# Node products of a four-layer graph network with several rows to one product

## The reference

```python
# layer two (attention): agg3 = mean * aw[0] + max * aw[1] + sum * aw[2]
ef = edge_label @ trans_weight                 # 8 labels to 64
att = sigmoid(leaky(x[row] * x[col] @ attention_weight) + leaky(ef @ edge_attention_weight))
out, opinion = agg3(x[col] * att, row), agg3(ef * att, row)
inn, inn_opinion = agg3(x[row] * att, col), agg3(ef * att, col)
cat = concatenate((out, opinion, inn, inn_opinion), axis=1)
y2 = cat @ weight + bias
...
# layer three (graph convolutions with self loops, norm = dinv[row] * ew * dinv[col])
x2 = relu(segment_sum(norm * (x @ w1)[row], col) + b1)      # 64 to 16
x3 = relu(segment_sum(norm * (x2 @ w2)[row], col) + b2)     # 16 to 32
x4 = relu(segment_sum(norm * (x3 @ w3)[row], col) + b3)     # 32 to 64
y3 = concatenate([x, x4], axis=1) @ lw + lb
```

## Time and profile before

| | |
|---|---|
| median of 3 runs | 15446.13 us (15444.47 to 15448.31) |
| the profiled execution's own time | 15444.99 us |
| its span, first to last instruction | 15443.3 us |
| mean granted TensorE clock | 0.689 |
| busy: POOL, DVE, PE | 70%, 59%, 47% of the span |
| products A, B, E, from the first transpose to the last result | 76.7, 34.6, 35.5 us |

### The profile page before, as it was taken

The page is one execution under the profiler, slowest core; times in us unless marked ns, Lnnn a source line. Parts: engine busy times, 40 slices in busy tenths (PEclk is TensorE's granted clock), DMA queues, the critical chain, the costliest instruction groups (busy, mean ns, idle before and its releaser), DMA issues. The chain is left out here.

```text
span 15443.3 us, 186434 instructions
## 1 busy us (share of the span) xinstructions
PE 7260.8 (47%) x53190; PEld 4887.6 (32%) x53190; DVE 9169.8 (59%) x21286; ACT 2508.3 (16%) x6533; POOL 10805.1 (70%) x10524
## 2 busy tenths in 40 slices
PE   3333333333320010001001355886787999699997
PEld 2222222222210000000000113786786555444443
DVE  5555554444444444444444796665665777587776
ACT  2222212222210000000000232111111111122222
POOL 6777777777767777777777301677777777588886
PEclk6555555555555555555555565998998999699998
DMA  2222223333323333333333574121211222122222
GB/s 81 70 71 72 71 64 95 103 103 101 103 83 94 94 99 94 93 99 94 93 97 96 202 272 149 39 44 37 43 43 36 48 49 50 26 72 72 71 73 60
DMA packets 631953, 1295.15 MB, mean 84 GB/s; under 512 B 219505, under 2 KB 366134, under 8 KB 606402
## 3 DMA queue, kind: packets, MB, share of 16 engines
q1 hardware_dynamic: 279776, 776.44, 14.4%
q0 software_dynamic: 337792, 456.35, 13.8%
q10 hardware_dynamic: 14337, 61.82, 1.1%
HBM read 623.75 MB, written 671.67 MB: 84 GB/s over the span
## 5 line engine op out<-in xcount | busy, mean ns | idle before, releaser
L521 POOL DMA_INDIRECT rows<-spline_table,index x3136 | 3181.4, 1014 | 1097.5 <-issue 973.9
L880 POOL DMA_INDIRECT rows<-gcn_table,index x2548 | 2515.9, 987 | 1008.1 <-issue 720.5
L920 PE MATMUL p_slots<-part,one_lo 128*128 128x208 bf16 (+1 forms) x25872 | 2973.8, 278 | 449.5 <-DVE one_lo L938 449.4
L920 PEld LDWEIGHTS p_slots<-part,one_lo 128*128 128x128 bf16 x25872 | 2372.6, 98 | 1050.2 <-DVE one_lo L938 492.9
L1116 POOL DMA_INDIRECT sent<-a_msg,a_place x1568 | 1625.9, 1037 | 478.0 <-issue 477.7
L1108 POOL DMA_INDIRECT a_rows<-att_table,a_index x1568 | 1486.2, 948 | 484.7 <-issue 477.2
L1170 PE MATMUL a_p_score<-tw_att,a_label 128*128 128x16 f32 x196 | 59.0, 381 | 3632.0 <-DMA a_label_row<-in_label_rows 3632.0
L1484 POOL DMA_INDIRECT e_rows<-soft_table,e_index x1176 | 1468.8, 1249 | 375.4 <-issue 328.8
L1526 PE MATMUL e_p_slots<-soft_part,e_one_lo 128*128 128x455 bf16 x8232 | 1644.7, 362 | 0.0
L1204 DVE TENSOR_TENSOR a_product<-a_rows,a_xdst 128x1024 f32<-128x1024 f32 x98 | 120.1, 1226 | 2067.2 <-DMA a_rows<-att_table,a_index 2067.2
L680 DVE TENSOR_TENSOR msg<-rows,weight 128x1024 f32<-128x1024 f32 x196 | 241.2, 1230 | 1814.2 <-DMA rows<-spline_table,index 1814.2
(11 more groups left out here) (430 smaller groups left out, 14929.7 us busy)
## 6 DMA issues: line engine op xcount, KB each, us to landing
running_dst<-a_run SPq DMA_DIRECT2D x98, 1600.0 KB
running_src<-s_run SPq DMA_DIRECT2D x98, 1600.0 KB
running<-e_run_rows SPq DMA_DIRECT2D x98, 656.0 KB
s_rows<-sent ACTq DMA_DIRECT2D x98, 584.0 KB, 7.0
keys<-key_rows SPq DMA_DIRECT2D x200, 256.0 KB, 3.3
running<-run SPq DMA_DIRECT2D x98, 520.0 KB
rows<-spline_table,index POOLq DMA_INDIRECT x3136
running<-run SPq DMA_DIRECT2D x98, 512.0 KB
```

The source lines that it names most:

```text
L521: pool.indirect_dma_start(out=rows[h][:, k, :], out_offset=None, in_=table, in_offset=offsets(index[h][:, k:k + 1])).then_inc(gathered[h], 16)
L880: pool.indirect_dma_start(out=rows[h][:, K + k, :], out_offset=None, in_=table, in_offset=offsets(index[h][:, k:k + 1])).then_inc(gathered ...
L920: ins = nc.tensor.matmul(to, one_lo[h][:, q, e:e + P], flat(part[:, q, :, :]), start=q == 0 and part_no == 0, stop=q == CLASSES - 1 and pa ...
```

## The change

`dense` gets a list `pack`, how many node rows of an input go to one product. For a pack of s it transposes s rows together (s times the width as columns) and multiplies with a weight tile that holds the weights s times on the block diagonal, so that one product gives s rows of the result side by side. Where seven isn't a multiple of s, the last block overlaps the one before it. A takes its label input seven rows at once (16 x 7 = 112 rows, 448 columns) and then adds the seven products of the other input, B and E take two rows (four blocks), C seven (one block, 112 rows, 224 columns), D four (two blocks, 256 columns). For this, 15 weight tiles' parts are loaded in place of 4, four tiles are cleared at the start, and the label weights are made on 112 rows and masked. `comb_lab` is no tile of its own any more but columns 184 to 199 of `agg_dst`, and `class_keys` uses columns 128 to 159 of each row of `agg_dst` as scratch.

```diff
-def dense(nc, sig, xs, weights, out, width, store=None, bias=None, block=None, scope=None, prepare=None, ready=0):
+def dense(nc, sig, xs, weights, out, width, store=None, bias=None, block=None, scope=None, prepare=None, ready=0, pack=None):
...
-        k_dims = [w.shape[0] for w in weights]
+        pack = pack or [1] * K
+        k_dims = [w.shape[0] // s for w, s in zip(weights, pack)]
+        starts = [[min(o, G - s) for o in range(0, G, s)] for s in pack]
...
-        xt = [sb(f"xt{k}_", [d, G, P]) for k, d in enumerate(k_dims)]
+        xt = [sb(f"xt{k}_", [s * d, len(o), P]) for k, (d, s, o) in enumerate(zip(k_dims, pack, starts))]
...
-                    ins = nc.vector.tensor_copy(flat(xt[k][b][:]), flat(tp[k][0:k_dims[k], 0:G, :]))
+                    ins = nc.vector.tensor_copy(flat(xt[k][b][:]), flat(tp[k][0:pack[k] * k_dims[k], 0:len(starts[k]), :]))
...
-                    for g in range(G):
-                        ins = nc.tensor.transpose(tp[k][0:k_dims[k], g, :], xin[k][b][:, g, :], sig["ident"][:])
+                    for m, o in enumerate(starts[k]):
+                        ins = nc.tensor.transpose(tp[k][0:pack[k] * k_dims[k], m, :], flat(xin[k][b][:, o:o + pack[k], :]), sig["ident"][:])
...
-                for g in range(G):
-                    for k in range(K):
-                        ins = nc.tensor.matmul(acc[b % ACCS][:, g, 0:width], xt[k][b][:, g, :], weights[k], start=(k == 0), stop=(k == K - 1))
+                to = acc[b % ACCS]
+                if K == 2 and pack[1] == G:
+
+                    nc.tensor.matmul(to[:, 0:G, 0:width], xt[1][b][:, 0, :], weights[1], start=True, stop=False)
+                    for g in range(G):
+                        ins = nc.tensor.matmul(to[:, g, 0:width], xt[0][b][:, g, :], weights[0], start=False, stop=g + 1 == G)
+                else:
+                    for m, o in enumerate(starts[0]):
+                        for k in range(K):
+                            ins = nc.tensor.matmul(to[:, o:o + pack[k], 0:width], xt[k][b][:, m, :], weights[k], start=(k == 0), stop=(k == K - 1))
...
-        w_ef, w_lab, twt = sb("w_ef", [C, 2, C]), sb("w_lab", [2 * LABELS, C]), sb("twt", [C, 3 * LABELS])
+        w_ef, w_lab, twt = sb("w_ef", [C, 2, C]), sb("w_lab", [GROUP_SLOTS * 2 * LABELS, GROUP_SLOTS, C]), sb("twt", [C, 3 * LABELS])
...
-        w1, w2, w3 = sb("gw1s", [C, 16]), sb("gw2s", [16, 32]), sb("gw3s", [32, C])
...
-        lws = [sb(f"lws{k}", [C, C]) for k in range(2)]
+        lws = [sb("lws0", [C, C])]
...
+        w1_two, w2_all, w3_four, lws1_two = sb("w1_two", [2 * C, 2, 16]), sb("w2_all", [GROUP_SLOTS * 16, GROUP_SLOTS, 32]), sb("w3_four", [P, 4, C]), sb("lws1_two", [2 * C, 2, C])
...
-            (w1[:], gw1), (w2[:], gw2), (w3[:], gw3), (gb[0][:], gb1.broadcast_to([P, 16])), (gb[1][:], gb2.broadcast_to([P, 32])),
-            (gb[2][:], gb3.broadcast_to([P, C])), (lws[0][:], lw[0:C, :]), (lws[1][:], lw[C:2 * C, :]), (lbs[:], lb.broadcast_to([P, C])),
+            *((w1_two[k * C:(k + 1) * C, k, :], gw1) for k in range(2)), *((w2_all[k * 16:(k + 1) * 16, k, :], gw2) for k in range(GROUP_SLOTS)),
+            *((w3_four[k * 32:(k + 1) * 32, k, :], gw3) for k in range(4)), (gb[0][:], gb1.broadcast_to([P, 16])), (gb[1][:], gb2.broadcast_to([P, 32])),
+            (gb[2][:], gb3.broadcast_to([P, C])), (lws[0][:], lw[0:C, :]), *((lws1_two[k * C:(k + 1) * C, k, :], lw[C:2 * C, :]) for k in range(2)), (lbs[:], lb.broadcast_to([P, C])),
...
-                    step(V.memset(w_labels[:], 0.0))
+                    for t in (w_labels, w1_two, w2_all, w3_four, lws1_two):
+                        step(V.memset(t[:], 0.0))
...
+                label_sides = [sb(f"label_side{k}", [C, GROUP_SLOTS, 2 * LABELS], F32, rows) for k in range(2)]
+                w_lab_at = sb("w_lab_at", [GROUP_SLOTS * 2 * LABELS, GROUP_SLOTS], F32, rows)
...
-                    TABLE, SHIFTED, DEGREES, MASKED = dve_s.base + 4, dve_s.base + 6, dve_s.base + 9, dve_s.base + 11
+                    LABEL_ROWS = GROUP_SLOTS * 2 * LABELS
+                    TABLE, SHIFTED, DEGREES, MASKED = dve_s.base + 4, dve_s.base + 6, dve_s.base + 9, dve_s.base + 14
...
-                        nc.tensor.matmul(ps[0:2 * LABELS, C:2 * C], twt[:, 0:2 * LABELS], w_ef[:, 0, :], start=True, stop=False)
-                        nc.tensor.matmul(ps[0:2 * LABELS, C:2 * C], twt[:, LABELS:3 * LABELS], w_ef[:, 1, :], start=False, stop=True).then_inc(pe_s.sem, 1)
+                        nc.tensor.matmul(ps[0:LABEL_ROWS, C:2 * C], flat(label_sides[0][:]), w_ef[:, 0, :], start=True, stop=False)
+                        nc.tensor.matmul(ps[0:LABEL_ROWS, C:2 * C], flat(label_sides[1][:]), w_ef[:, 1, :], start=False, stop=True).then_inc(pe_s.sem, 1)
...
+                        for k in range(2):
+                            step(V.tensor_copy(label_sides[k][:], repeat(twt[:, k * LABELS:(k + 2) * LABELS], GROUP_SLOTS)))
+                        step(V.tensor_reduce(w_lab_at[:], sig["ident"][0:LABEL_ROWS, 0:LABEL_ROWS].rearrange("p (k l) -> p k l", l=2 * LABELS), AX.X, ALU.add))
...
-                        step(V.tensor_copy(w_lab[:], ps[0:2 * LABELS, C:2 * C]))
+                        step(V.tensor_tensor(w_lab[:], repeat(ps[0:LABEL_ROWS, C:2 * C], GROUP_SLOTS), spread(w_lab_at[:], C), ALU.mult))
...
-            comb_dst, comb_lab = sb("comb_dst", [P, J, 2 * C], F32, tmp), sb("comb_lab", [P, J, 2 * LABELS], F32, tmp)
+            comb_dst = sb("comb_dst", [P, J, 2 * C], F32, tmp)
+
+            comb_lab = agg_dst[:, :, RUN - 2 * LABELS:RUN]
...
-                    in_class = flat(agg_dst[:])[:, 0:T]
-                    step(V.tensor_copy(src_key[:, 0:T], src_lo[:, 0:T]))
+                    def by_row(t):
+                        return t[:, 0:T].rearrange("p (j c) -> p j c", j=J)
+
+                    in_class, key, low, high = agg_dst[:, :, 2 * C:2 * C + T // J], by_row(src_key), by_row(src_lo), by_row(src_hi)
+                    step(V.tensor_copy(key, low))
...
-                        step(V.tensor_scalar(in_class, src_hi[:, 0:T], q * CLASS - 0.5, None, ALU.is_gt))
-                        step(V.scalar_tensor_tensor(src_key[:, 0:T], in_class, float(P * q), src_key[:, 0:T], ALU.mult, ALU.add))
-                        step(V.scalar_tensor_tensor(src_hi[:, 0:T], in_class, -float(CLASS * q), src_hi[:, 0:T], ALU.mult, ALU.add))
+                        step(V.tensor_scalar(in_class, high, q * CLASS - 0.5, None, ALU.is_gt))
+                        step(V.scalar_tensor_tensor(key, in_class, float(P * q), key, ALU.mult, ALU.add))
+                        step(V.scalar_tensor_tensor(high, in_class, -float(CLASS * q), high, ALU.mult, ALU.add))
...
-            dense(nc, sig, [comb_src, comb_lab], [w_src[:], w_lab[:]], y, C, bias=y)
+            dense(nc, sig, [comb_src, comb_lab], [w_src[:], flat(w_lab[:])], y, C, bias=y, pack=(1, GROUP_SLOTS))
...
-                dense(nc, sig, [agg[2]], [w3[:]], x4, C, bias=gb[2][:], block=block, scope=scope, prepare=own_part)
-
-            dense(nc, sig, [xs], [w1[:]], x2, 16)
+                dense(nc, sig, [agg[2]], [flat(w3_four[:])], x4, C, pack=(4,), bias=gb[2][:], block=block, scope=scope, prepare=own_part)
+
+            dense(nc, sig, [xs], [flat(w1_two[:])], x2, 16, pack=(2,))
...
-            convolve(1, second_table, lambda block, scope, own_part: dense(nc, sig, [agg[1]], [w2[:]], x3, 32, bias=gb[1][:], block=block, scope=scope, prepare=own_part))
+            convolve(1, second_table, lambda block, scope, own_part: dense(nc, sig, [agg[1]], [flat(w2_all[:])], x3, 32, pack=(GROUP_SLOTS,), bias=gb[1][:], block=block, scope=scope, prepare=own_part))
...
-            dense(nc, sig, [x4], [lws[1][:]], y, C, bias=y)
+            dense(nc, sig, [x4], [flat(lws1_two[:])], y, C, bias=y, pack=(2,))
```

## The result

| | before | after |
|---|---|---|
| median of the runs, us | 15447.22 (15444.47 to 15449.35, 4 runs) | 15351.72 (15347.81 to 15354.81, 4 runs) |
| profiled execution, us (its span) | 15444.99 (15443.3) | 15350.33 (15348.6) |

The ratio of the runs is 0.9938, with a 95% interval of 0.9921 to 0.9955: the changed kernel is faster by 95.5 us. The five products gave more than was forecast, and some 9 us of it did not reach the end.

What follows compares the result with a forecast made beforehand. TensorE was taken to bound A, B and E, the chain after the last gather C and D. Savings of 31.1 + 15.6 + 5.2 + 12.4 + 16.1 = 80.4 us gave 15366 us, range 15340 to 15397.

Steps and rivals of the forecast that it cites:

- A: Attention layer's sources product, w_src with w_lab; forecast to take 45.5 us, 31.1 saved.
- B: Product w1 at the graph layer's entry; forecast 15.6 us saved.
- E: Product lws[1] at the graph layer's end; forecast 16.1 us saved, or 15.4 if its 128-column records cost more.
- C: Product w2 beside the fetch, counted only after the last gather; forecast 5.2 us saved.
- D: Product w3 beside the fetch, counted only after the last gather; forecast 12.4 us saved.
- D's step that the gather takes the bound over: In the w3 product, the last gather, not TensorE, becomes late, so 12.4 us of 16 are saved.
- The price of a record at 0.50: TensorE's fp32 records at the low clock: 0.208 us up to 128 columns, 0.76 for 448, 0.43 for 256, 0.38 for 224.
- 22 x 0.208 + 2 x 0.76 = 6.10 us: Time per group in A after the change: 8 transposes, 14 w_src records and 2 wide label records.
- the clock rises: Rival: TensorE's clock goes up; A would lose 19 us more, B and E 8 each, giving 15331; 7%.
- three other rivals: Chain in series, 31 us lost, 9%; packed records priced as full, 81 us, 3%; long passes' gathers retimed, 15482 us, 3%.
- the chain in series: Rival: each multiply waits for its copy; B and E periods near 4, A 7.5, 31 us lost, 15397; 9%.
- What was costed at nothing: Slower class-key comparisons (2.4 us), eleven weight loads, four memsets, extra VectorE steps; all taken as hidden beside other work.

Runs made afterwards that it cites:

- b_wide: Changed kernel with B reading each weight column four times (128 columns a record, not 32); slower chip, 19019.44 us, ratio 0.9913; B 14.5 us.
- a_by_rows: Changed kernel with A as before the change, labels multiplied row by row; slower chip, 19048.22 us, ratio 0.9913; A 75.1 us.
- a_narrow_label: Changed kernel with A's labels still turned once for seven rows but multiplied row by row, 14 records of 64 columns; A 39.5 us.
- e_narrow: Changed kernel with E computing only 16 of 64 result columns, 32 columns a record instead of 128; E 18.9 us instead of 14.9.
- keys_flat: Changed kernel with the class keys' steps over flat tiles as before, comparison output contiguous; 15323.99 us against 15324.5.
- after_again: Changed kernel once more, unaltered, beside runs of the kernel before on one chip; 15324.5 us, ratio 0.9934.
- a_no_label: Changed kernel without A's two wide label-product records, labels still copied and transposed; A 24.5 us.
- more_packed: Changed kernel with the first layer's two w0 products on two rows at once and B reading weights four times; 15299.35 us, ratio 0.9919.

## Why the prediction came out as it did

- **What bounds the stages: right.** In A, B and E the engine without rest is TensorE before and after, C and D end by the chain behind the last gather. D's step that the gather takes the bound over shows in VectorE's 4.34 us of waiting; without that step 16 would have been forecast where 12.6 came.
- **The price of a record at 0.50: right.** A's group was put at 6.10 us and took 6.11 where the clock was still low (b_wide), B's at 2.50 and took 2.46; 224 and 256 columns were priced well enough for C to end 5.9 us after the last gather's issue (6.3) and D 8.9 (9). B, C and D missed by at most 0.5 us each. The wide pair of w_lab starts at 9571.99 and the next product at 9573.48: 0.75 us a record, where 0.76 had been taken. The 0.37 us for 448 columns, estimated from the formula for the low clock in the Trainium skill ("TensorE: Matmul & The Clock Gate", Back-to-back issue gap), is half of that for an fp32 record here.
- **A: the mis-sized term, by its clock.** 31.1 was forecast and 49.5 came. The step that failed is "22 x 0.208 + 2 x 0.76 = 6.10 us" for every group. It holds only at 0.50. In the profile the first period is 9575.13 - 9570.26 = 4.87 us, the clock rising in it, and the others 3.15: 1.2 and five times 3.0 us less, and 2 us less in the last multiply, make the 18. The prediction had seen records at both paces in the old A, and gave a rise throughout 7%. It did not foresee that the new A would hold the high clock where the old one kept falling back, which a_by_rows and a_narrow_label show.
- **E: the same, smaller.** 16.1 forecast, 20.6 measured, the period 1.5 us from the third group on. B was taken as evidence for E. It was none: B stays low with 32 columns a record and rises with 128, E rises with 128 and stays low with 32 (b_wide, e_narrow). The Trainium skill's "TensorE: Matmul & The Clock Gate", Part 1, says that a busy TensorE gets the full clock. E's two forms do not bear that out as the profile counts busy: in the first 7 us from the first transpose they are equally busy, 6.13 us with 128 columns and 6.12 with 32 (changed kernel, e_narrow), and only the first rose.
- **The rival *the clock rises* happened in half**: in A and E, not in B. Its conditions were tested against B alone. The three other rivals did not happen: the periods are TensorE's own sum, packed records of 128 columns cost 0.24 us, the long gathers' mean is 1014 ns before and after. The price given to the chain in series, 31 us, does not follow from its own periods: 12 of B and E at 1.5 us more and six of A at 1.4 make 26.
- **What was costed at nothing: right.** Comparisons take 1.79 us (1.8); the keys are sent at 9544.60, the last gather is at 9547.95: the cover of 7 us shrank to 3.4 and still covers. The 3 us either way on POOL came out as 1.3 us gained (keys_flat). The added weight loads end near 4420 instead of 4414, still ahead of the store at 4446.89, and the first cast of the opening starts at 10.14 instead of 10.05.
- **The sum against the whole.** 104.1 us in the stages, 94.7 in the span, 80.4 forecast. That a clock rising in part stays inside the range was reasoned. That the number came within 14 us was in part luck: the stages gave 23.7 us more than forecast, and the passes nobody edited took 9.4 longer. On the chip of after_again the medians differ by 101.8 us, 21 more than forecast. Most of those 9.4 lie in the softmax pass, which differs by more than that between two profiles of the changed kernel; the second pair, on one chip, leaves 2.6 us. That any of it belongs to the change was not shown.
- **Open.** What makes the clock rise in A's first multiply in one execution and in the second in another (27.15 and 29.6 us), and why the old A swings, was not settled. Nor was what decides for a rise in general: columns decided in B and E, but w_dst and a_no_label's A, so alike, went different ways.

## What to carry to other kernels

Price a product in the fp32 records that it issues: here, at the low clock, one of 32 or 64 columns cost 0.21 to 0.22 us and one of 128 only 0.24, so stacking small node rows into one tall operand with block-diagonal weights saves turns and records. Work out such a stage at both of TensorE's clock levels, and don't take the level seen in one product for another whose records differ, as was done here from B to E. When TensorE gets faster, look at once for the single accumulator, the last gather or the copy that is late next.

## What the runs showed of the hardware that was not expected

- More columns in the same number of records made a product faster: B went from 18.9 to 14.5 us when each record had 128 columns instead of 32, as the clock rose from 0.50 to 1.00 in its second multiply. Records of 128 columns took 0.24 us at the low clock and 0.13 at the high one.
- Operands of 16 and 128 rows in turns cost 0.307 us a record at 0.50, operands of 112 and 128 rows in turns 0.21. An alternation of that kind is worth avoiding in itself.
- At the start of the span the clock's column can't be taken at its word. In the first product it reads 1.00 throughout, though its records of 128 columns take 0.239 us, as elsewhere at 0.50; in more_packed it reads 1.00 too while eight records fall from 3.62 to 1.99 us. There the records' own durations tell the clock.
